# Graph attention on one core: the mask of a block made by VectorE at the end of its turn in place of ScalarE in the middle

## The reference

```python
def _transformer_conv(x, src, dst, wq, bq, wk, bk, wv, bv, ws, bs):
    q = (x @ wq + bq).reshape(n, H, C); k = ...; v = ...
    alpha = jnp.einsum('ehc,ehc->eh', q[dst], k[src]) / sqrt(C)
    amax = jax.ops.segment_max(alpha, dst, num_segments=n)
    ex = jnp.exp(alpha - amax[dst])
    denom = jax.ops.segment_sum(ex, dst, num_segments=n)
    a = ex / (denom[dst] + 1e-16)
    out = jax.ops.segment_sum(a[:, :, None] * v[src], dst, num_segments=n)
    return out.mean(axis=1) + x @ ws + bs
```

## Time and profile before

| | us |
|---|---|
| median of 3 runs | 5740.71 |
| lowest and highest | 5737.53, 5747.76 |
| the profiled execution's own time | 5738.76 |
| its span in the trace | 5736.5 |

### The profile page before, as it was taken

One profiled execution on the slowest core, in us unless ns is written; L12 is line 12 of the kernel. 1 busy time (PEld: TensorE's weight loads), 2 busy tenths in 40 slices (PEclk: granted clock), 3 DMA queues, 4 the chain that ended last, 5 costly groups with the idle time before them and its releaser, 6 DMA issues. The chain is left out here.

```text
span 5736.5 us, 107111 instructions
## 1 busy us (share of the span) xinstructions
PE 3956.4 (69%) x31282; PEld 2987.8 (52%) x31283; DVE 3804.2 (66%) x9916; ACT 2218.3 (39%) x2892; POOL 1395.5 (24%) x1703
## 2 busy tenths in 40 slices
PE   4667676825445444545456888888888879997997
PEld 2222266824444444444444444444444449995996
DVE  7999967755556555565633555544555568886887
ACT  2433433011111111111112555555555547874885
POOL 0000000017777777777771000000000000000000
PEclk8999988955555555555556999988999969996998
DMA  1111144722222222222111111101111121112110
GB/s 38 68 57 61 65 149 158 277 49 56 64 59 59 54 59 59 64 59 60 47 50 40 58 57 57 57 30 64 57 57 57 51 65 41 51 34 71 51 46 29
DMA packets 235223, 370.66 MB, mean 65 GB/s; under 512 B 169839, under 2 KB 175973, under 8 KB 235142
## 3 DMA queue, kind: packets, MB, share of 16 engines
q1 hardware_dynamic: 190006, 264.11, 14.2%
q0 software_dynamic: 41536, 85.08, 5.6%
q10 hardware_dynamic: 3600, 20.48, 0.9%
HBM read 292.58 MB, written 76.99 MB: 64 GB/s over the span
## 5 line engine op out<-in xcount | busy, mean ns | idle before, releaser
L1069 POOL DMA_INDIRECT en_got<-edge_q,en_now x1296 | 1302.0, 1005 | 408.9 <-issue 325.9
L1258 PE MATMUL en_t<-ident,en_got 128*128 128x128 f32 x1296 | 361.1, 434 | 957.3 <-DVE en_got L1152 957.3
L1296 ACT ACTIVATE en_hid<-en_t 128x512 f32<-128x512 f32 x324 | 193.4, 597 | 1648.9 <-DMA en_got<-edge_q,en_now 1402.7
L1258 PEld LDWEIGHTS en_t<-ident,en_got 128*128 128x128 f32 x1296 | 231.5, 217 | 1035.7 <-DVE en_got L1152 1035.7
L1266 PEld LDWEIGHTS en_o<-en_w2s,en_hid 128*128 128x128 f32 x2592 | 582.8, 333 | 0.0
L1266 PE MATMUL en_o<-en_w2s,en_hid 128*128 128x64 f32 x2592 | 577.4, 411 | 0.0
L1152 DVE TENSOR_TENSOR en_got<-en_got,p (+1 forms) x324 | 224.5, 693 | 494.2 <-ACTq L1290 461.4
L456 PE MATMUL cnt_ps<-cnt_hot_l,cnt_hot_k 128*128 128x400 bf16 x1600 | 358.6, 355 | 192.8 <-DVE cnt_hot_l L421 179.0
L1849 PE MATMUL r1s_ps<-hp,r1s_bits 128*128 128x193 bf16 x5000 | 423.5, 248 | 26.6 <-DVE r1s_bits L1802 13.6
L1849 PE MATMUL r0s_ps<-hp,r0s_bits 128*128 128x193 bf16 x5000 | 423.5, 248 | 26.7 <-DVE r0s_bits L1802 13.6
L1849 PEld LDWEIGHTS r1s_ps<-hp,r1s_bits 128*128 128x128 bf16 x5000 | 418.1, 98 | 32.0 <-issue 31.6
(11 more groups left out here) (393 smaller groups left out, 7619.5 us busy)
## 6 DMA issues: line engine op xcount, KB each, us to landing
en_got<-edge_q,en_now POOLq DMA_INDIRECT x1296
count_panels<-cnt_panel SPq DMA_DIRECT2D x25, 800.0 KB, 3.4
type_panels<-cnt_panel SPq DMA_DIRECT2D x25, 800.0 KB, 4.8
c0s_panel<-count_panels SPq DMA_DIRECT2D x25, 800.0 KB, 4.4
count_rows<-c0s_rows ACTq DMA_DIRECT2D x25, 800.0 KB, 3.5
c1s_panel<-count_panels SPq DMA_DIRECT2D x25, 800.0 KB, 5.7
c1s_rows<-count_rows SPq DMA_DIRECT2D x25, 800.0 KB, 7.3
en_raw<-count_panels SPq DMA_DIRECT2D x25, 800.0 KB
```

The costliest lines, as they stand in the source:

```text
L1069: pool.indirect_dma_start(out=got[:, i, j, :], out_offset=None, in_=k.q[:, :], in_offset=bass.IndirectOffsetOnAxis(ap=now[i][:, j:j + 1], ...
L1258: last = pe.transpose(tps[i % 2][:, j * P:(j + 1) * P], got[:, i, j, :], k.ident[:, :])
L1296: act.activation(hid[i % 2][:, :], tps[i % 2][:, :], ACT.Relu).then_inc(lined, 1)
```

## The change

ScalarE's `mask` goes away, with the tile `huge` (the constant 1e30) and the semaphore `huge_ok`. VectorE gets a `mask` that computes (count == 0) * 1e30 in place with one `tensor_scalar`. Its first two calls stand ahead of the first veils of block 0; the call for block w + 2 stands at the very end of turn w, after `find_top` of block w + 1.

```diff
-        huge = sb("huge", [P, 1], F32)
...
-            def mask(w, u):
-                act.wait_ge(mask_in[u], (w - u) * 8 + 16)
-                act.activation(no_row[u][:, :], no_row[u][:, :], ACT.Relu, bias=huge[:, 0:1],
-                               scale=NEG).then_inc(masked, 1)
...
-                    if c == 1 and following is not None:
-                        mask(w + 2, u)
-            act.wait_ge(huge_ok, 1)
-            mask(0, 0)
-            mask(1, 1)
             windows(act, window)
...
-            v.memset(huge[:, :], -NEG).then_inc(huge_ok, 1)
+            def mask(w, u):
+
+                wait_alone(v, mask_in[u], (w - u) * 8 + 16, passed_v)
+                v.tensor_scalar(no_row[u][:, :], no_row[u][:, :], 0.0, -NEG, ALU.is_equal,
+                                ALU.mult).then_inc(masked, 1)
+
+            mask(0, 0)
+            mask(1, 1)
             for i in range(NS):
                 veil(0, 0, i)
             find_top(0, 0)
...
                     find_top(w + 1, 1 - u)
+                if following is not None:
+                    mask(w + 2, u)
             windows(v, window)
```

More of the change, by code:

```diff
@@ L1412, in attention @@
         mask_in = [sem(f"mask_in{u}") for u in range(2)]
-        huge_ok = sem("huge_ok")
         q_ok, masked, scored, veiled, top_ok, expd, weighed = map(
```

## The result

The changed kernel takes 5529.48 us in the median of 4 runs (5528.06 to 5532.9), where the kernel before took 5741.47 us in 4 runs. The ratio is 0.9627, with a 95% interval of 0.9614 to 0.9639: the change takes 3.7% off the time. The forecast was 5526 us, in a range of 5510 to 5552. The profiled execution took 5529.14 us with a span of 5527.1, against 5738.76 and 5736.5 before, so 209.4 us of span have gone.

What follows compares the result with a forecast made beforehand. ScalarE's mask, the exponential and copies behind it, then TensorE at half clock were taken to bound each block. Blocks save 220.6 us, head and clock lose 3.2 each: 214.2 less, 5524.6 profiled, 5526 us expected, range 5510 to 5552.

Steps and rivals of the forecast that it cites:

- What bounds the kernel: Attention blocks, 29.0 us on average: ScalarE's mask delays the last exponential and copies, then TensorE runs at half clock.
- The new block, built of two measured parts, 24.17 us: Loop block without ScalarE's mask: 17.14 us before its place, from the loop, plus 7.03 us behind it, from block 23.
- The 0.20 us kept for the loop: Part before the mask's place: 17.14 us in the loop against 16.94 in written-out block 23, for register work in waits.
- VectorE's mask, 0.99 us, hidden: End of a turn: the mask takes 0.99 us inside VectorE's 3.42 us idle time after `find_top`; load wait costs nothing.
- The head, 3.2 us: Start of each layer: both masks precede the first veil, first exponential 1.6 us late; 3.2 us lost in two layers.
- The clock at the start of a block, one fall in each layer, 3.2 us: Short TensorE waits opening a block: one clock fall of 1.6 us per layer, 3.2 us lost; bounds none to 74.
- The sum: Whole kernel: 220.6 - 3.2 - 3.2 = 214.2 us less, 5524.6 us profiled, 5526 us expected.
- The first, many falls: TensorE's clock falls at the start of many blocks: 5597 us for all 46, 5548 for a third; chance 0.09.
- The second: Block 23 is short for another reason, having little DMA traffic and no GpSimd copy: 131 us saved, 5613 us; chance 0.05.
- The third: The mask is slow on VectorE, 3.49 us: blocks lose 9 us, the head 5 more, 5540 us; chance 0.03.
- the fourth: VectorE's mask waits for its load, holding the next block's first `weigh`: slower than before, 5970 us; chance 0.02.
- The fifth: The change does nothing, because something else ends at the same time as the mask; chance 0.01.

## Why the prediction was right, step by step

- *What bounds the kernel.* Right. The mask's place in ScalarE's queue set the block, by its length and by the clock. All 3200 columns put back bring 29 us back, the pieces at other places do not, and the filled gap separates 2.84 us of wait from 2.0 us of clock.
- *The new block, built of two measured parts, 24.17 us.* Right: 24.18. The 0.20 us kept for the loop were right too, since block 23, which is written out, takes 23.97 us beside it. Block 0 was put at 25.05 and 25.55 us and came to 25.57 and 25.50. So the old block 23 was a fair sample.
- *VectorE's mask, 0.99 us, hidden.* Right in both: 0.99 us, and leaving it out changes the blocks by nothing. The wait for the load cost nothing inside the blocks.
- *The head, 3.2 us.* The mechanism was right, the term mis-sized: 4.2 us. The first veil came 1.7 us later after the first load's issue (9.4 against 7.7), near the 1.6 forecast, but the exponential came 2.1 and 2.2 later. The forecast had left out that TensorE, too, stands longer ahead of its third pair of scores and has its full clock back later, 0.4 us in each layer.
- *The clock at the start of a block, one fall in each layer, 3.2 us.* The mechanism was right, the term mis-sized: six falls of 1.53 us, 9.2 us. The prediction had three blocks of the old trace to go by, two without a fall and one with it, and the one fall in each layer was a guess between them. The Trainium skill, "TensorE: Matmul & The Clock Gate", section "A second HAM failure mode: psum-queue depth-cycling", says that short idles between groups of matmuls can make the clock swing. The runs agree with it in kind (filled waits, no falls) and put its share here at 6 of 46 blocks, far from the upper bound that the prediction drew from it.
- *The sum.* 220.6 us were forecast for the blocks and 210.8 came. Nearly all of the difference is the six falls, 9.2 us, which the prediction had in a term of its own at 3.2. On the other side stand 2.9 us of gain around the layers, which no step had. Against the profiled execution the forecast was 5524.6 and 5529.1 came: 6.0 us for the falls, 1.0 for the head and 0.5 for block 0 missing in it, less the 2.9, which is 4.6 us against the 4.5 measured. That the 2.9 us stood against the three was luck. The range's lower end, by its own terms, is 5526 - 9 - 3 = 5514 us and not 5512; nothing hangs on it.
- *The rivals.* The first, many falls, holds in part: six, not fifteen. The second is refuted by blocks that have their DMA and GpSimd copy (share 0.20, copy of 0.78 us) and still take 24.18 us. The third fell with the 0.99 us, the fourth with the mask's wait in the changed kernel, 0.43 us behind `find_top` and not for its load. The fifth fell with the result.

## What to carry to other kernels

An engine that is busy 60% of the time can still set the length of a loop: look at what stands in its queue ahead of the one instruction for which others wait. Price such an instruction by its length plus what TensorE loses in clock after the gap, here 2.84 and 2.0 us for an instruction of 2.95, and first try to cut it into pieces that fit its own engine's waits; in total that did as much here as the other engine. A turn of the loop that lacks the step, here the last prepared block, is the best forecast of the loop without it, except for rare events: two samples tell little of one that comes in 6 of 46.

## What the runs showed of the hardware that was not expected

The price of a gap on TensorE is no smooth function of its length. 0.75 us more in each block gave 22 falls of the clock, 1.42 us more gave seven, nothing more gave six. With 1.42 us more, six of the seven are blocks 1 to 6 of the second layer, one behind the other; with nothing more they lie six or seven blocks apart. What decides it stays open. Six transposes of 0.88 us in all removed the falls and left the ordinary block at 24.18 us.

GpSimd's copy of the next queries takes longer, though nothing in it was changed. Its group in the changed kernel:

```profile
L1449 POOL COPY a0s_qw<-qt x25: 283/777/858, 3116.4 to 3669.4; 128x128 f32 x22, 128x128 f32<-128x128 f32 x3
```

Its median is 777 ns where one was 0.29 us in the earlier trace rows. In the shorter block it falls together with VectorE's `weigh` of 640 columns, as the timeline of block 14 shows: the copy starts at 3498.60, and the `weigh` beside it from 3499.16 takes 0.90 us where the one ahead takes 0.82. The kernels with work on ScalarE at the old place show 0.29 or 0.30 again, and the one without a mask shows 0.78, so it goes with the overlap and not with the mask. The Trainium skill, "SBUF — State Buffer", section "Who interferes with whom", says that GpSimd and VectorE share a pair of SBUF ports under an exclusive lock; the trace agrees in kind, with a copy that is 0.5 us longer. It costs nothing here: the ordinary block is 24.18 us with the longer copy, and the kernel with a mask in pieces has the same block and the same copy.
